# Projected blocks leave PSUM by a copy on ACT, and DVE's rotary steps read the copy in two parts

## The chip, the cores and the metric

One core of one Trainium2 chip. The metric is the device time of one execution in microseconds (us). The kernel before: 2270.76 us, the median of 3 runs (2270.74 to 2271.02). A shorter time is better.

The engines are named as in the profile: PE (TensorE, matmuls) with PEld (its weight loads), DVE (VectorE), ACT (ScalarE), POOL (GpSimd) and SP (SyncE, here the queue that issues the DMAs).

## The reference

4 x 1024 tokens of width 256 go through three stages, each added to its input: half an expert layer, attention, half the same expert layer again.

```
x = x + 0.5 * experts(layernorm(x))
x = x + attention(layernorm(x))
x = x + 0.5 * experts(layernorm(x))

experts:   32 experts of inner width 96, silu(gate) * up, then down; top 8 by softmax,
           cut where the renormalised sum passes 0.8, the weights renormalised
attention: q = x Wq^T (16 heads of 16), k = x Wk^T, v = x Wv^T (4 heads of 16)
           q = q * cos + rotate_half(q) * sin ; k the same      (v is not rotated)
           softmax(q k^T / 4) v, then Wo^T
```

All tensors are float32. The rotary step pairs each element of the first half of a head with one of the second half.

## The kernel before, in words

Everything is one long order of 384 slots, written out per engine. A slot d is one pair of expert chunks for a group of 512 tokens: PE computes gate and up (L1211) for slot d + 1 and down (L1229) for slot d - 1. 24 slots make a group, 192 a layer. Each float32 product is made of three float16 passes (high x high, high x low, low x high). The token groups of the first expert layer are also projected for attention, one group after another: in group k, slot s = d mod 24, three *join* events project group g = k - 1: first keys and values in one block (64 + 64 rows), then two blocks of queries (128 rows each). They stand in slots 8, 10, 13 for the first two groups and in 10, 12, 14 for the other six (join_slots).

From slot 64 on, *visits* are woven in: each gives PE two score matmuls for the row maxima (L1241, halves of 512 keys) and two for the exponentials (L1253), DVE two maxima (L960, one per half, each frees the bank of the next score matmul of its half), ACT two exponentials (L691). A slot has two or three visits. Every second visit or so PE also does a set of value matmuls (L1274).

The order in a slot, PE: gate, visit, up, visit, down, (visit), event. DVE: maxima of the first visit, gated (L937, once tanh is there), product (L945), maxima of the second visit, normalisation and routing pieces that the slot number names, event. POOL: low part of the hidden block (L606), rotary low part (L588), weighting by the expert weights (L601, released by the product). ACT: tanh (L668), exponentials, high part (L675), rotary high part (L682), exponentials.

PSUM has 8 banks, all in use. An event of PE writes its result into bank 7 early in the kernel and, while the value matmuls hold that bank (slots 79 to 311), into the bank of up (B_U) or gate (B_G). So the next up-projection waits for whoever reads the event's result (`taken`).

A join before the change, on DVE at the end of its slot (function join, L910 to L927): for the first block a transpose of the values out of PSUM (L918); then the cosine product into rb (L922) and the two sine products with halves swapped into turned (L923, L925), all three with the PSUM block as one operand and a table in SBUF as the other. The third one signals j_taken, which frees the bank. In the middle of the next slot, after the product, the sum rb + turned (L932) signals rope_done. One slot later ACT takes the high float16 part of rb (L682) and POOL the low part (L588), which signals qo_lo_done; then SP stores both. rb and turned are single buffers, so a join waits for qo_lo_done of the one before. In group slots 6, 7, 9 and 11 DVE has four normalisation pieces for the next group; the one in slot 11 is four operations of L839 (norm, piece 3). SP loads the cosine and sine tables of group g in slot 1 (function tables).

Of the kernel before, what the change touches and what calls it, by code (L numbers as in the profile page):

```python
# [7 lines left out]
ALU = mybir.AluOpType  # L8
ACT = mybir.ActivationFunctionType
# [6 lines left out]
P = 128  # L16
# [17 lines left out]
K_ROWS = KV * HD  # L34
# [82 lines left out]
JOINS = QB + 1  # L117
# [13 lines left out]
def join_slots(k):  # L131

    return () if k not in range(1, GROUPS + 1) else (8, 10, 13) if k - 1 in JOINS_BY_PE else (10, 12, 14)
# [66 lines left out]
def build(nc, x, wgu, wd, wg, wq, wk, wv, wo, ident_c, ktab_c, kneg_c, out):  # L200
    with ExitStack() as ctx:
# [32 lines left out]
        turned = sb("turned", [P, GROUP])  # L234
# [55 lines left out]
        v_turned = vb_f[K_ROWS:, :]  # L290
# [17 lines left out]
        PS = ctx.enter_context(nc.psum_tensor("PS", [P, 8, 512], F32))  # L308
# [10 lines left out]
        def bank16(b):  # L319
# [33 lines left out]
        j_done, j_taken, rope_done, qo_hi_done, qo_lo_done = (  # L353
            sem("j_done"), sem("j_taken"), sem("rope_done"), sem("qo_hi_done"), sem("qo_lo_done"))
        v_set, tab_in, vb_out, qo_out = sem("v_set"), sem("tab_in"), sem("vb_out"), [sem(f"qo_out{i}") for i in range(JOINS)]
# [37 lines left out]
        def _(sp):  # L393
# [4 lines left out]
            for k in range(2 * KT):  # L398
                n = n_gu // (2 * KT)
# [44 lines left out]
            def tables(g):  # L444

                cols = slice(g % 2 * GROUP, g % 2 * GROUP + GROUP)
                if g:
                    sp.wait_ge(j_taken, JOINS * g)
                for t, v in enumerate((kcos, ksin)):
                    sp.dma_start(v, ktab_c[t, :, cols]).then_inc(tab_in, 16)  # L450

# [189 lines left out]
        def _(act):  # L641
# [52 lines left out]
            def event(d, i):  # L694

                bank = event_bank(d, i)
                name, n, j = EVENTS[d][i]
                if name in ("p_hi", "p_lo"):
                    take_rows(norm_of_join(n), n % 2, name == "p_lo", bank)
                if name in ("t_hi", "t_lo"):  # L700
                    take_rows(norm_of_group(n), n % 2, name == "t_lo", bank)
# [64 lines left out]
        def _(dve):  # L766
# [140 lines left out]

            HALF = 2.0 ** 3 / XW

            def join(g, piece, bank):  # L910
                dve.wait_ge(j_done, JOINS * g + piece + 1)
                J = PS[:, bank, :]
                n, m = P if piece else K_ROWS, JOINS * g + piece
                if piece == 0:
                    dve.wait_ge(tab_in, 32 * (g + 1))
                    if g:
                        dve.wait_ge(vb_out, g * 64)
                    dve.transpose(v_turned, J[K_ROWS:, :]).then_inc(v_set, 1)  # L918
                if m:
                    dve.wait_ge(qo_lo_done, m)  # L920
                link.many((
                    dve.scalar_tensor_tensor(rb[0:n, :], J[0:n, :], HALF, kcos[0:n, :], ALU.mult, ALU.mult),  # L922
                    dve.scalar_tensor_tensor(turned[0:n // 2, :], J[n // 2:n, :], -HALF, ksin[n // 2:n, :],  # L923
                                             ALU.mult, ALU.mult)))
                dve.scalar_tensor_tensor(turned[n // 2:n, :], J[0:n // 2, :], HALF, ksin[0:n // 2, :],  # L925
                                         ALU.mult, ALU.mult).then_inc(j_taken, 1)
                dve.wait_ge(v_set, g + 1)  # L927

            def rope_sum(g, piece):
                n, m = P if piece else K_ROWS, JOINS * g + piece  # L930
                dve.wait_ge(j_taken, m + 1)
                dve.tensor_tensor(rb[0:n, :], rb[0:n, :], turned[0:n, :], ALU.add).then_inc(rope_done, 1)  # L932

            def gated(d):
# [92 lines left out]
            def event(d, i):  # L1027

                bank = event_bank(d, i)
                name, n, j = EVENTS[d][i]  # L1030
                if name == "logits":
                    route(n, 0, bank)
                if name == "join":
                    join(n, j, bank)
                if name == "out_y":
                    add_outputs(n, j, bank)

# [57 lines left out]
            for d in range(-1, SLOTS + 2):  # L1095
                k, s = divmod(d, PER_GROUP)
                if d % PER_HALF == 1 and d > 1:
                    add_dense(d // PER_HALF - 1)
                if (d, 0) in VISIT:
                    visit(VISIT[d, 0])  # L1100
                if d + 1 < SLOTS:
                    gated(d + 1)
                    product(d + 1)
                if (d, 0) in VISIT:
                    unit_ends(VISIT[d, 0])
                if s - 1 in join_slots(k):
                    rope_sum(k - 1, join_slots(k).index(s - 1))
                if d == -1 or d == 0:
                    split_piece(1, d + 1)
                if d in D_LOW_AT:  # L1110
                    split_d(D_LOW_AT.index(d) + 1)
                if d in (2, 3, 5, 6):
                    split_piece(2 + d // 5, (d - 2) % 3)
                if d == 8:
                    split_small()
                if d == SPLIT_BY - 1:
                    dve.memset(vst_f, 0.0).then_inc(ones_set, 1)
                    dve.wait_ge(ones_set, 1)
                    dve.memset(vst[:, :, :, HD:HD + 1], XW / 2.0 ** 6).then_inc(ones_set, 1)
                if (d, 1) in VISIT:  # L1120
                    visit(VISIT[d, 1])
                if len(EVENTS[d]) > 1:
                    event(d, 1)
                if (d, 2) in VISIT:
                    unit_ends(VISIT[d, 1])
                    visit(VISIT[d, 2])
                if d in OUT_AT:
                    normalise(OUT_AT.index(d))
                if d - 2 in OUT_AT:
                    turn_back(OUT_AT.index(d - 2))  # L1130
                if 1 <= k <= GROUPS and 2 <= s < 6:
                    if s == 2:
                        dve.wait_ge(x_done, 2 * k)
                    norm(norm_of_join(k - 1), k - 1, s - 2, k + 1)
                if 0 <= k < PREPS - 1:
                    if s in steps_of_norm(k)[0]:
                        norm_of(k + 1, steps_of_norm(k)[0].index(s))
                    if s == T_LOGITS + 1:
                        route(k + 1, 1)
                        route(k + 1, 2)  # L1140
                    if s == T_LOGITS + 2:
                        route(k + 1, 3)
                        route(k + 1, 4)
                    if s == T_LOGITS + 3:
                        route(k + 1, 5)
                        route(k + 1, 6)
                if EVENTS[d]:
                    event(d, 0)
                if (d, 2) in VISIT:
                    unit_ends(VISIT[d, 2])  # L1150
                elif (d, 1) in VISIT:
                    unit_ends(VISIT[d, 1])
# [282 lines left out]
```

## Time and profile before

| | us |
|---|---|
| median of 3 runs | 2270.76 |
| the profiled execution | 2270.94 |
| its span, first to last instruction | 2269.1 |
| PE busy | 2200.3 (97%) |
| DVE busy | 1626.9 (72%) |
| ACT busy | 1166.9 (51%) |
| POOL busy | 1072.5 (47%) |

Busy is the time in which an engine has at least one instruction running; the ends of matmuls are modelled. TensorE's granted clock is full speed over the whole span but for its first moments. An idle time of an engine counts only where PE, which is busy nearly all the time, waits for it in the end.

### The profile page before, as it was taken

How to read it: one execution, taken by the hardware profiler on the slowest of the kernel's cores; microseconds unless marked ns; L12 is line 12 of the kernel's file. 1: busy time of each engine (PE TensorE's matmuls, PEld its weight loads, DVE VectorE, ACT ScalarE, POOL GpSimd, SP SyncE). 2: the span in 40 equal slices, each digit the busy share in tenths (PEclk: the TensorE clock that was granted, in tenths of full speed). 3: DMA queues.
4: the chain of work that ended last, by engine and by line, in shares of the span. 5: the costliest groups of instructions: out<-in, count | busy, mean ns of one | idle time of the engine just before them, and what ended most of it. 6: DMA issues, size and time to landing. Idle time of an engine off the chain costs nothing.

```text
span 2269.1 us, 47149 instructions
## 1 busy us (share of the span) xinstructions
PE 2200.3 (97%) x18794; PEld 1487.7 (66%) x18794; DVE 1626.9 (72%) x3203; ACT 1166.9 (51%) x1885; POOL 1072.5 (47%) x908
## 2 busy tenths in 40 slices
PE   3999999999999999999999999999999999999998
PEld 2888875556565565565566566566655665688887
DVE  7756678887887877787877877777777754454543
ACT  4433331666556556565556565566656556433332
POOL 1767654444444444444434443434344334466655
PEclk9999999999999999999999999999999999999999
DMA  5211121011111120110211111010110110101010
GB/s 222 80 41 37 39 58 31 23 42 31 35 31 43 33 51 25 34 37 24 53 41 32 31 36 32 20 42 16 26 47 6 29 32 20 30 26 40 22 40 20
DMA packets 157956, 88.50 MB, mean 39 GB/s; under 512 B 103588, under 2 KB 149924, under 8 KB 156968
## 3 DMA queue, kind: packets, MB, share of 16 engines
q1 hardware_dynamic: 157592, 85.45, 14.1%
q8 instruction: 148, 2.42, 0.4%
q14 instruction: 72, 0.59, 0.1%
q10 hardware_dynamic: 144, 0.03, 0.0%
HBM read 63.14 MB, written 11.80 MB: 33 GB/s over the span
## 4 chain that ended last, share of the span: by engine, by line
PE 89%; DVE 7%; DMA 1%; issue 1%; ACT 1%; POOL 1%; SPq 0%; POOLq 0%; DVEq 0%
PE PS L1211 43%; PE PS L1229 21%; PE PS L1241 11%; PE PS L1274 10%; DVE arena L960 2%; PE PS L1193 1%; PE PS L1303 1%; DMA X<-wd 1%; PE PS L1253 1%; DVE arena L937 1%; DVE arena L945 1%; PE PS L1179 0%; DVE turned L923 0%; DVE turned L925 0%; DVE arena L922 0%
## 5 line engine op out<-in xcount | busy, mean ns | idle before, releaser
L1211 PE MATMUL PS<-XT,WGU 128*128 128x256 f16 x9216 | 1112.0, 273 | 14.2 <-DVE turned L925 8.8
L1211 PEld LDWEIGHTS PS<-XT,WGU 128*128 128x128 f16 x9216 | 875.9, 98 | 236.9 <-issue 129.9
L606 POOL TENSOR_TENSOR arena<-arena 128x512 f16<-128x512 f32 x384 | 451.2, 1175 | 1065.9 <-ACT arena L675 1065.9
L960 DVE TENSOR_REDUCE arena<-PS 128x1 f32<-128x512 f32 x1024 | 656.5, 684 | 269.3 <-PE PS L1241 265.4
L691 ACT ACTIVATE arena<-PS,fac 128x512 f32<-128x512 f32 x1024 | 647.4, 685 | 270.7 <-PE PS L1253 270.5
L668 ACT ACTIVATE arena<-PS,fac 128x512 f32<-128x512 f32 x384 | 264.4, 689 | 771.7 <-PE PS L1211 771.7
L1229 PE MATMUL PS<-WD,arena 128*128 128x256 f16 x4608 | 568.3, 273 | 2.6 <-POOL arena L606 2.4
L601 POOL TENSOR_TENSOR arena<-arena 128x512 f32<-128x512 f32 x384 | 501.7, 1306 | 85.9 <-DMA arena<-ce_scratch 44.5
L1229 PEld LDWEIGHTS PS<-WD,arena 128*128 128x128 f16 x4608 | 430.4, 98 | 145.6 <-issue 94.6
L937 DVE SCALAR_TENSOR_TENSOR arena<-arena,PS 128x512 f32<-128x512 f32 x384 | 261.2, 680 | 247.4 <-ACT arena L668 246.6
L1241 PE MATMUL PS<-arena 48*128 48x512 f16 x1024 | 318.9, 382 | 14.9 <-DVE arena L960 12.8
L1253 PE MATMUL PS<-arena 50*128 50x512 f16 x1024 | 315.9, 382 | 0.0
L945 DVE SCALAR_TENSOR_TENSOR arena<-arena,PS 128x512 f32<-128x512 f32 x384 | 263.8, 687 | 29.7 <-PE PS L1211 12.8
L675 ACT ACTIVATE arena<-arena 128x512 f16<-128x512 f32 x384 | 242.0, 630 | 16.1 <-POOL arena L601 15.9
L1274 PE MATMUL PS<-arena 128*32 128x512 f32 x2048 | 246.2, 598 | 0.0
L1241 PEld LDWEIGHTS PS<-arena 48*128 48x128 f16 x1024 | 62.1, 94 | 216.6 <-issue 124.7
L1274 PEld LDWEIGHTS PS<-arena 128*32 128x32 f32 x2048 | 53.4, 109 | 103.6 <-issue 93.4
L1253 PEld LDWEIGHTS PS<-arena 50*128 50x128 f16 x1024 | 63.6, 93 | 15.1 <-issue 10.9
L583 POOL TENSOR_TENSOR XS<-XN,XS 128x1024 f16<-128x1024 f32 x23 | 49.0, 2131 | 0.0
L839 DVE TENSOR_SCALAR XN<-X,mv,rstd 128x256 f32<-128x256 f32 x96 | 43.8, 517 | 0.0
L843 DVE BATCH_NORM_STATS2 stats<-X 128x6 f32<-128x256 f32 x96 | 33.4, 411 | 3.1 <-DMA X<-x 3.1
L1303 PE MATMUL PS<-WO,arena 128*128 128x256 f16 x256 | 33.3, 273 | 0.2 <-DVE arena L937 0.2
(117 smaller groups left out, 729.5 us busy)
## 6 DMA issues: line engine op xcount, KB each, us to landing
arena<-ce_scratch SPq DMA_DIRECT2D x256, 128.0 KB, 3.2
arena<-wgu SPq DMA_DIRECT2D x4, 1536.0 KB, 13.4
arena<-q_scratch SPq DMA_DIRECT2D x192, 32.0 KB
arena<-ktab_c SPq DMA_DIRECT2D x16, 256.0 KB, 4.0
q_scratch<-arena SPq DMA_DIRECT2D x32, 128.0 KB, 1.8
out<-X SPq DMA_DIRECT2D x8, 512.0 KB, 3.0
X<-wd SPq DMA_DIRECT2D x2, 1536.0 KB, 24.0
X<-x SPq DMA_DIRECT2D x1, 3072.0 KB, 12.1
```

Source lines behind the costliest of these rows:

```text
L601: pool.tensor_tensor(t, t, c, ALU.mult).then_inc(w_done, 1)
L606: pool.tensor_tensor(hs[1][:, d % HS, :], tw[d % 2], hs[0][:, d % HS, :], ALU.subtract).then_inc(lo_done, 1)
L668: act.activation(z_f, PS[:, B_G, :], ACT.Tanh, scale=F_TANH).then_inc(z_done, 1)
L691: act.activation(pex[:, v % RING * 2 + half, :], PS[:, B_EXP + half, :], ACT.Exp, scale=F_EXP).then_inc(exp_done, 1)
L937: dve.scalar_tensor_tensor(z_f, z_f, 1.0, PS[:, B_G, :], ALU.add, ALU.mult).then_inc(v_done, 1)
L945: dve.scalar_tensor_tensor(tw[d % 2], z_f, G_U_UP, PS[:, B_U, :], ALU.mult, ALU.mult).then_inc(t_done, 1)
L960: dve.tensor_reduce(mx[:, half * REP * QT + c:half * REP * QT + c + 1], PS[:, B_MAX + half, :], AX_X, ALU.max).then_inc(max_taken, 1)
L1211: ins = pe.matmul(PS[:, b, j * HALF_G:(j + 1) * HALF_G], WGU[w][:, kt, part * CHUNKS + c + j, :], XT[r][:, k % 2, kt, half * HALF_G:(half ...
L1229: ins = pe.matmul(PS[:, B_Y, i * HID:(i + 1) * HID], hs[r][:, d % HS, at:at + P], WD[w][:, d % PER_HALF * 2 + j, :], start=(first and j == ...
L1241: pe.matmul(PS[:, B_MAX + half, :], qst[64 * par:64 * par + 48, slot, i, t * P:(t + 1) * P], kst[64 * par:64 * par + 48, slot, half * 512: ...
L1253: pe.matmul(PS[:, B_EXP + n % 2, :], kst[64 * par:64 * par + 50, slot, k * P:(k + 1) * P], qst[64 * par:64 * par + 50, slot, head // 2, ha ...
L1274: ins = pe.matmul(PS[32 * head:32 * head + 32, B_O, :], vst[:, u % 2, k, :], pex[:, (2 * q + r // 2) % RING * 2 + r % 2, :], start=(k == 0 ...
```

## The change

ACT copies the whole block from PSUM into rb, at the event's place in its own order, and signals j_taken. DVE no longer has a join at the end of the slot. In the middle of the next slot, where the sum stood, DVE now computes the two sine products from rb (rope_partners); at the end of that next slot, after the event, it transposes the values out of rb (first block), multiplies rb by the cosine in place and adds turned (rope_sum). SP's table load waits for rope_done instead of j_taken.

```diff
@@ sync: tables(g)
-                    sp.wait_ge(j_taken, JOINS * g)
+                    sp.wait_ge(rope_done, JOINS * g)
@@ scalar: event(d, i)
+                if name == "join":
+                    m = JOINS * n + j
+                    act.wait_ge(j_done, m + 1)
+                    if m:
+                        act.wait_ge(qo_lo_done, m)
+                    act.activation(rb, PS[:, bank, :], ACT.Copy).then_inc(j_taken, 1)
@@ vector
-            def join(g, piece, bank):
-                dve.wait_ge(j_done, JOINS * g + piece + 1)
-                J = PS[:, bank, :]
+            def rope_partners(g, piece):
                 n, m = P if piece else K_ROWS, JOINS * g + piece
+                dve.wait_ge(j_taken, m + 1)
                 if piece == 0:
                     dve.wait_ge(tab_in, 32 * (g + 1))
+                link.many((
+                    dve.scalar_tensor_tensor(turned[0:n // 2, :], rb[n // 2:n, :], -HALF, ksin[n // 2:n, :],
+                                             ALU.mult, ALU.mult),
+                    dve.scalar_tensor_tensor(turned[n // 2:n, :], rb[0:n // 2, :], HALF, ksin[0:n // 2, :],
+                                             ALU.mult, ALU.mult)))
+
+            def rope_sum(g, piece):
+                n = P if piece else K_ROWS
+                if piece == 0:
                     if g:
                         dve.wait_ge(vb_out, g * 64)
-                    dve.transpose(v_turned, J[K_ROWS:, :]).then_inc(v_set, 1)
-                if m:
-                    dve.wait_ge(qo_lo_done, m)
-                link.many((
-                    dve.scalar_tensor_tensor(rb[0:n, :], J[0:n, :], HALF, kcos[0:n, :], ALU.mult, ALU.mult),
-                    dve.scalar_tensor_tensor(turned[0:n // 2, :], J[n // 2:n, :], -HALF, ksin[n // 2:n, :],
-                                             ALU.mult, ALU.mult)))
-                dve.scalar_tensor_tensor(turned[n // 2:n, :], J[0:n // 2, :], HALF, ksin[0:n // 2, :],
-                                         ALU.mult, ALU.mult).then_inc(j_taken, 1)
-                dve.wait_ge(v_set, g + 1)
-
-            def rope_sum(g, piece):
-                n, m = P if piece else K_ROWS, JOINS * g + piece
-                dve.wait_ge(j_taken, m + 1)
+                    dve.transpose(v_turned, rb[K_ROWS:, :]).then_inc(v_set, 1)
+                    dve.wait_ge(v_set, g + 1)
+                link(dve.scalar_tensor_tensor(rb[0:n, :], rb[0:n, :], HALF, kcos[0:n, :], ALU.mult, ALU.mult))
                 dve.tensor_tensor(rb[0:n, :], rb[0:n, :], turned[0:n, :], ALU.add).then_inc(rope_done, 1)
@@ vector: event(d, i)
-                if name == "join":
-                    join(n, j, bank)
@@ vector: the slot loop, after gated, product and unit_ends
                 if s - 1 in join_slots(k):
-                    rope_sum(k - 1, join_slots(k).index(s - 1))
+                    rope_partners(k - 1, join_slots(k).index(s - 1))
@@ vector: the slot loop, after the event
+                if s - 1 in join_slots(k):
+                    rope_sum(k - 1, join_slots(k).index(s - 1))
```

## Rows read from the trace of the kernel before

**Rows 1.** The page: span and PE's busy time.
```profile
span 2269.1 us, 47149 instructions
...
PE 2200.3 (97%) x18794; PEld 1487.7 (66%) x18794; DVE 1626.9 (72%) x3203; ACT 1166.9 (51%) x1885; POOL 1072.5 (47%) x908
```
**Rows 2.** PE's waits, 400 to 1320 us: total, times, longest.
```profile
PE PS L1211 <- DVE turned L925: 8.8, 13, 1.2
PE PS L1241 <- DVE arena L960: 7.8, 20, 0.9
```
**Rows 3.** All waits: DVE's for the projection matmuls.
```profile
DVE arena L922 <- PE PS L1193: 16.5, 14, 1.8
...
DVE arena L918 <- PE PS L1193: 7.9, 7, 1.8
```
**Rows 4.** The page's groups, tanh on ACT: busy us, mean ns, idle before.
```profile
L668 ACT ACTIVATE arena<-PS,fac 128x512 f32<-128x512 f32 x384 | 264.4, 689 | 771.7 <-PE PS L1211 771.7
```
**Rows 5.** Timeline 603 to 617 us, DVE then PE: start us, length us.
```profile
603.04 0.72 DVE L918 STREAM_TRANSPOSE arena<-PS 64x512 f32<-64x512 f32 x1 [1.02 <-PE PS L1193]
...
605.93 1.29 DVE L960 TENSOR_REDUCE arena<-PS 128x1 f32<-128x512 f32 x2
...
612.67 1.28 DVE L960 TENSOR_REDUCE arena<-PS 128x1 f32<-128x512 f32 x2
...
604.24 0.39 PE L1241 MATMUL PS<-arena 48*128 48x512 f16 x1
...
606.05 1.47 PE L1211 MATMUL PS<-XT,WGU 128*128 128x256 f16 x12 [1.20 <-DVE turned L925]
...
614.75 0.38 PE L1241 MATMUL PS<-arena 48*128 48x512 f16 x1
```
**Rows 6.** Timeline 1098 to 1108 us, DVE then PE.
```profile
1099.11 1.29 DVE L960 TENSOR_REDUCE arena<-PS 128x1 f32<-128x512 f32 x2 [0.69 <-PE PS L1241]
...
1105.32 1.27 DVE L960 TENSOR_REDUCE arena<-PS 128x1 f32<-128x512 f32 x2
...
1106.65 0.39 PE L1241 MATMUL PS<-arena 48*128 48x512 f16 x1 [0.21 <-DVE arena L960]
```
**Rows 7.** Timeline 188 to 191 us; then line L601: min/median/max ns.
```profile
188.27 0.68 DVE L932 TENSOR_TENSOR arena<-arena,turned 64x512 f32<-64x512 f32 x1
188.43 1.65 POOL L601 TENSOR_TENSOR arena<-arena 128x512 f32<-128x512 f32 x1 [0.62 <-DVE arena L945]
188.87 1.22 DVE L852 TENSOR_TENSOR nw<-rs 128x4 f32<-128x4 f32 x1
...
190.12 0.16 DVE L853 TENSOR_TENSOR nw<-nw,var 128x4 f32<-128x4 f32 x1
...
L601 POOL TENSOR_TENSOR arena<-arena x384: 1256/1269/2789, 49.9 to 2260.2; 128x512 f32<-128x512 f32 x192
```
**Rows 8.** Timeline 1263 to 1275 us, DVE then PE.
```profile
1263.57 1.29 DVE L960 TENSOR_REDUCE arena<-PS 128x1 f32<-128x512 f32 x2 [0.69 <-PE PS L1241]
...
1271.67 1.29 DVE L960 TENSOR_REDUCE arena<-PS 128x1 f32<-128x512 f32 x2
...
1274.20 0.38 PE L1241 MATMUL PS<-arena 48*128 48x512 f16 x1
```
**Rows 9.** Timeline 1130 to 1136 us (a third block), DVE then PE.
```profile
1130.77 1.08 DVE L932 TENSOR_TENSOR arena<-arena,turned 128x512 f32<-128x512 f32 x1
1131.77 2.47 DVE L960 TENSOR_REDUCE arena<-PS 128x1 f32<-128x512 f32 x4
1135.26 1.29 DVE L960 TENSOR_REDUCE arena<-PS 128x1 f32<-128x512 f32 x2 [1.02 <-PE PS L1241]
...
1133.10 0.39 PE L1241 MATMUL PS<-arena 48*128 48x512 f16 x1 [0.21 <-DVE arena L960]
```
**Rows 10.** Timeline 620 to 629 us (a second block), PE then DVE.
```profile
620.80 0.38 PE L1211 MATMUL PS<-XT,WGU 128*128 128x256 f16 x2 [0.47 <-DVE turned L925]
...
628.02 1.29 DVE L960 TENSOR_REDUCE arena<-PS 128x1 f32<-128x512 f32 x2 [1.65 <-PE PS L1241]
```

## The prediction

> **What bounds the kernel now.** I read the page first: PE is busy in 2200.3 of 2269.1 us [rows 1]. So only what holds PE up can move the time, and the next view is PE's waits inside the stretch where attention runs beside the expert slots (400 to 1320 us) [rows 2]. The gate/up matmuls wait 8.8 us in 13 places for DVE's last rotary step (L925), because a projected block lies in the bank that the next up-projection wants. The score matmuls wait another 7.8 us in 20 places for DVE's row maxima (L960): so DVE runs close to PE's pace here, and a delay of DVE turns into a delay of PE. Third, DVE's own waits: 24.4 us for the projection matmuls, in 21 places [rows 3].
>
> **What goes.** The ACT copy takes over the release of the bank. Its price is a 128x512 PSUM read on ACT, 0.69 us by the tanh of the same shape, and ACT is idle before that tanh (771.7 us over the kernel, ended by the gate matmuls) [rows 4]. The next gate matmuls alone take some 1.5 us after the projection (twelve of them 1.47 [rows 5]), so the copy is finished before the up matmuls start: the 8.8 us go. Six of these stalls are followed by a 0.1 us stall of a score matmul that goes with them (no row shown): -9.4 us at most. I put the copy at 0, hidden by ACT's wait for the gate matmuls; without that cover it would be 0.7 us for each of the 18 blocks that share a bank with them, 13 us. The extra wait in front of the copy (qo_lo_done) is one DVE had at the same place; behind it on ACT stands the next tanh. It was met in time before and I cost it at 0. The table load of SP waits for rope_done instead of j_taken: it has ten slots to spare, 0.
>
> **What moves on DVE.** Per block three operations of some 0.7 us (for the first block of a group a transpose of 0.72 too [rows 5]) ran at the end of the projection's slot, in time in which DVE had little else, since PE was doing the projection and the gate. Now two of them stand in the middle of the next slot, and the others with the sum at its end. No work is saved: five instructions before, five after (four for a later block). What changes is that DVE can't begin them until it has done the next slot's first maxima, gate and product. I write M0 for the first maxima of the slot after that; PE's second score matmul of the visit that follows needs both.
>
> *First block of a group, third query-time group (603 to 617 us).* [rows 5] Four operations, 603.04 to 605.93, 2.9 us. The first maxima start at 605.93, though their scores were written at 604.24 + 0.39 = 604.63: 1.3 us of that is won back when the operations leave. They come back before M0: so M0 at 612.67 moves by 2.9 - 1.3 = 1.6 us, plus the collision below (0.9): 2.5 us. The M0 pair then ends at 612.67 + 2.5 + 1.28 = 616.45, and PE's second score matmul, which began at 614.75, can't begin before 616.5. That is +1.8 us at this place, the saved 1.2 us stall [rows 5] already inside, because I compare clock times. The cause is that this slot also holds the four normalisation steps of L839, so DVE has no idle time between the two rows of maxima.
>
> *The worst case (1099 to 1107 us).* [rows 6] Here DVE waited 0.69 us for the scores before its first maxima: the rotary steps had been wholly hidden, nothing is won back. M0 moves by 2.9 + 0.9 = 3.8 us from 1105.32 to 1109.1, ends at 1110.4, and PE's second score matmul was at 1106.65: +3.8 us.
>
> **The collision.** The rotary steps used to read one operand from PSUM. From the copy, the three products read two SBUF tensors, as the sum L932 already did. The trace shows what this does beside POOL [rows 7]: L932 starts at 188.27; POOL's weighting L601, released by the product just before, takes 1.65 us where its median is 1.27 (it begins after L932 is through); and the next all-SBUF DVE operation, L852 on 4 columns, takes 1.22 us where its neighbour L853 of the same size takes 0.16: it ends with L601, at 190.09. Now the two partner steps stand exactly there, behind the product. The first takes L932's part, the second L852's: it ends about 0.5 us (0.69 less 0.16) after L601, at 190.6, where two free steps would end at 188.27 + 2 x 0.69 = 189.65. So 0.9 us more for each of 24 blocks. Ends: 0 (if the second step wins against POOL) and 1.5 us (L932 itself was held to 1.08 us in one place, where another POOL operation was in flight [rows 9], so 0.4 more, and 0.2 for a hit at the cosine step now and then, a guess). I take 0.9, the nearest row. Where unit_ends' small steps stand between the product and the partners (one group), POOL gets through beforehand: 0 there.
> The Trainium skill, SBUF — State Buffer, section Who interferes with whom, says that a DVE instruction with two SBUF inputs and a GpSimd instruction that reads SBUF exclude each other for a whole instruction, whichever started first; the trace agrees in the three rows just read. By a per-operation reading of that rule alone every one of the three steps could be held; by the rows only the one behind another is.
>
> **The sum.** First blocks, six groups in the attention stretch: 1.8 and 3.8 from above; the last group, DVE idle before its maxima as in the worst case, M0 at 1271.67 + 3.8, end 1276.75, PE's second score matmul at 1274.20: +2.6 [rows 8]. Three more of the pattern, read in the same way: +1.7, +1.6 (the one without a collision) and +0.6 (DVE has 1.2 us of idle time in that stretch). Together +12.1.
> Second blocks: the stall of 0.47 us goes and M0 is late by 1.6 + 0.9 less what is won back (1.2), while DVE was idle 1.65 us there [rows 10]: nearly covered. The six give from -0.3 to +0.5, I take +0.6 together.
> Third blocks: only 0 to 0.5 us is won back. In the worst-shaped one the sum was held to 1.08 us by POOL, two partner steps with the second behind L601 come to 0.7 + 0.9 = 1.6 us more, and PE's score matmul waits already (at 1133.10, after 0.21 us): +1.6 [rows 9]. The others by the same reading: +2.1, +0.8, +0.7, +0.6, -0.5. Together +5.3, of which I keep 4.3, as DVE's idle time behind (1.02 us [rows 9]) takes part of it.
> The two groups before attention starts: DVE waits for a projection 24.4 / 21 = 1.2 us on the mean [rows 3] and lets it pass, but here PE's slot has no visits and is short, so gate waits for gated now and then; between 0 and 2 us each, I take 1, together 2.
> Sum: 12.1 + 0.6 + 4.3 + 2.0 = +19.0 us. The profiled execution took 2270.94 us, 0.18 over the median 2270.76. Forecast 2289.8, say 2290 us.
>
> **Rivals.**
> *A, the moved work finds room (faster).* The mechanism: DVE is no longer late for the first maxima, PE reaches the next slot earlier, and the idle time that DVE has in it (24.4 us were spent waiting for projections [rows 3]) absorbs the five steps. Then the 9.4 us go and nothing comes: 2261.5. For it: DVE is busy 72% only, and the idle times of 0.69 to 1.65 us [rows 6, 10]. Against it: between the two rows of maxima of rows 5 DVE has none. It decides if less than half of the first-block lateness appears, which needs M0 to be late by under 1 us.
> *B, no collision.* The second partner step wins against POOL or reads no shared path. Then every first block is 0.9 cheaper (five of them, 4.5), the second and third blocks about 8 together, and the early groups 1: 19.0 - 13.5 = +5.5, so 2276.4. Against it: L852 behind L601 [rows 7].
> *C, ACT becomes late too.* rope_high stands on ACT before the next slot's second pair of exponentials and now waits for a sum that comes 2.5 to 3.8 us later; the score matmuls for exp would wait 0.5 to 1 us in each first block: +5 on top, 2295.
> By the same page of the Trainium skill (SBUF — State Buffer, Who interferes with whom) the loser of a collision waits the whole of the other's instruction: were each of the three steps a loser, an estimate would be a further 1.2 us in the crowded slots, still under C's end.
> A rival that the change doesn't do what it says I don't see: the bank is released by a semaphore on another engine, and that is all it needs.
>
> **Chances.** Forecast case (2283 to 2294) 0.55; A 0.12; B and cases between B and the forecast (2273 to 2283) 0.25; C 0.08. Faster by over 0.2% (4.5 us, about what can be told from no change): A, 0.12. Within it: what of B lies under 2275.3, 0.12. Slower: 0.76. The range reaches down to 2271, where A's lesser forms begin, and up to 2297.
>
> **What would show it.** No wait of L1211 for a rotary step; ACT copy near 0.69 us; one partner step near 0.7 and the other near 1.6 us; PE's wait for L960 between 400 and 1320 us up from 7.8 to some 25 to 35 us, with stalls of 1.5 to 4 us at a first block's second slot. I am wrong if the partner steps both take 0.7 us (B), or if L960 stalls stay under 15 us (A).

## The result: 2332.3 us, slower by 2.7%

| | before | after |
|---|---|---|
| median | 2270.76 us | 2332.3 us (2330.35 to 2333.22, 5 runs) |
| the profiled execution | 2270.94 us | 2332.3 us |
| its span | 2269.1 us | 2330.5 us |
| PE busy | 2200.3 us | 2222.4 us |

The ratio is 1.027, 95% interval [1.0255, 1.0285]. The forecast was 2290 us, at most 2297: the direction was right, and the loss is 61.5 us where 19 were forecast.

PE's waits of the whole kernel, after: total, times, longest.

```profile
PE PS L1246 <- DVE arena L965: 51.0, 78, 3.1
...
PE PS L1216 <- DVE arena L942: 12.4, 11, 2.8
```

L965 is the row maximum (L960 before), L942 is gated (L937 before). In the trace of before the same two waits over the whole kernel are 12.8 and 2.3 us; the wait for the third rotary step, 8.8 us in 13 places [rows 2], is gone. So PE waits 38.2 + 10.1 - 8.8 = 39.5 us longer. That is not all of the 61.5. The rest is in the clock. The core row (span, mean granted clock) was 1.000 before and is now:

```profile
core 0: 2330.5 us, clock 0.992
```

0.8% of 2330.5 us is 19 us. Stretches of the trace of after around two equal stalls of PE show where it goes (the columns are the stretch, its length, busy us of PE, PEld, DVE, ACT, POOL, then the granted clock, DMA share, GB/s):

```profile
205.00:209.00 4.00, 3.82 (x20) 2.80 (x21) 2.08 (x4) 2.34 (x4) 3.73 (x3) 0.57 0.28 89
312.00:316.00 4.00, 3.64 (x34) 3.27 (x35) 3.02 (x5) 2.63 (x4) 3.56 (x3) 1.00 0.33 101
```

Both start at the end of a stall of 2.8 us behind gated, as PE's timeline of after shows:

```profile
205.18 1.18 PE L1216 MATMUL PS<-XT,WGU 128*128 128x256 f16 x6 [2.78 <-DVE arena L942]
...
312.36 0.83 PE L1216 MATMUL PS<-XT,WGU 128*128 128x256 f16 x6 [2.79 <-DVE arena L942]
```

After the first, TensorE ran at the lower level, 1.2 GHz, for most of 4 us and did 20 matmuls; after the second it stayed at 2.4 GHz and did 34. The trace has eleven such stretches of 3.4 us inside the span, each beginning within 2 us of the end of a stall of PE of 1.4 to 3.1 us. Of the 18 stalls of that length between 180 and 1360 us, the other seven brought none. The trace of before has neither such a stall nor such a stretch there (in both traces the clock falls once more in the last 2 us, as the work ends). At half speed each costs 1.7 us, 18.8 in all. 39.5 + 18.8 = 58.3 of the 61.5 us; the last 3 us I did not trace.

The worst case of before [rows 6], after the change, DVE (start us, length us):

```profile
1137.72 1.29 DVE L965 TENSOR_REDUCE arena<-PS 128x1 f32<-128x512 f32 x2 [4.05 <-PE PS L1246]
...
1140.96 0.68 DVE L924 SCALAR_TENSOR_TENSOR turned<-arena 32x512 f32<-32x512 f32 x1
1141.67 1.64 DVE L926 SCALAR_TENSOR_TENSOR turned<-arena 32x512 f32<-32x512 f32 x1
1143.35 1.29 DVE L965 TENSOR_REDUCE arena<-PS 128x1 f32<-128x512 f32 x2
1144.55 1.37 DVE L845 TENSOR_SCALAR XN<-X,mv,rstd 128x256 f32<-128x256 f32 x4
1145.96 0.71 DVE L934 STREAM_TRANSPOSE arena<-arena 64x512 f32<-64x512 f32 x1
1146.70 1.47 DVE L936 SCALAR_TENSOR_TENSOR arena<-arena 64x512 f32<-64x512 f32 x1
1148.20 0.68 DVE L937 TENSOR_TENSOR arena<-arena,turned 64x512 f32<-64x512 f32 x1
1148.81 1.27 DVE L965 TENSOR_REDUCE arena<-PS 128x1 f32<-128x512 f32 x2
```

POOL in the same stretch, and PE's score matmuls that wait for the two pairs of maxima:

```profile
1141.01 1.76 POOL L601 TENSOR_TENSOR arena<-arena 128x512 f32<-128x512 f32 x1 [0.18 <-DVE arena L950]
1146.48 1.15 POOL L606 TENSOR_TENSOR arena<-arena 128x512 f16<-128x512 f32 x1 [3.70 <-ACT arena L675]
...
1144.10 0.39 PE L1246 MATMUL PS<-arena 48*128 48x512 f16 x1 [1.51 <-DVE arena L965]
...
1149.55 0.39 PE L1246 MATMUL PS<-arena 48*128 48x512 f16 x1 [3.05 <-DVE arena L965]
```

Read it from the product's end, 1140.9. The first sine product (L924) takes 0.68 us. POOL's weighting L601, released by the product, stretches from 1.27 to 1.76 us. The second sine product (L926) ends 0.5 us after L601, as forecast. But the cosine product (L936) too takes 1.47 us, beside L606, which starts 0.2 us before it. DVE has no idle moment between the first maxima and 1150, and PE loses 1.51 + 0.21 us and then 3.05 + 0.21 us.

The rotary steps of all blocks (ns: min/median/max; L924 and L926 the sine products, L937 the sum, L936 the cosine product, L703 the ACT copy):

```profile
L924 DVE SCALAR_TENSOR_TENSOR turned<-arena x24: 680/1026/1193, 187.3 to 1354.3; 64x512 f32<-64x512 f32 x16, 32x512 f32<-32x512 f32 x8
L926 DVE SCALAR_TENSOR_TENSOR turned<-arena x24: 681/1642/1658, 188.2 to 1355.5; 64x512 f32<-64x512 f32 x16, 32x512 f32<-32x512 f32 x8
L937 DVE TENSOR_TENSOR arena<-arena,turned x24: 683/692/1527, 193.0 to 1359.1; 128x512 f32<-128x512 f32 x16, 64x512 f32<-64x512 f32 x8
...
L936 DVE SCALAR_TENSOR_TENSOR arena<-arena x24: 648/682/1470, 192.3 to 1358.4; 128x512 f32<-128x512 f32 x16, 64x512 f32<-64x512 f32 x8
...
L703 ACT ACTIVATE arena<-PS x24: 597/597/598, 183.8 to 1350.1; 128x512 f32<-128x512 f32 x24
```

To place the loss I compared the start of each slot's gate matmuls in both traces. The growth of the difference, by block and its next slots, sums to 61.3 us:

| | forecast (us) | measured (us) | of it clock stretches, number: x 1.7 us | without them |
|---|---|---|---|---|
| first blocks, six later groups | 12.1 | 27.6 | 5: 8.5 | 19.1 |
| second blocks | 0.6 | 8.6 | 2: 3.4 | 5.2 |
| third blocks | 4.3 | 12.5 | 3: 5.1 | 7.4 |
| the two groups before attention | 2.0 | 12.6 | 1: 1.7 | 10.9 |
| sum | 19.0 | 61.3 | 11: 18.7 | 42.6 |

### The profile page after: what moved, and what is told of

The parts are those of the page before. It is cut to its first block, busy times and chain, and to the rows that moved or that the text cites. A ratio compares the mean times of both kernels' runs of the same rounds, so it can differ in the third digit from the quotient of the medians.

```text
span 2330.5 us, 47175 instructions
## 1 busy us (share of the span) xinstructions
PE 2222.4 (95%) x18794; PEld 1494.6 (64%) x18794; DVE 1662.0 (71%) x3203; ACT 1181.7 (51%) x1909; POOL 1073.1 (46%) x908
## 4 chain that ended last, share of the span: by engine, by line
PE 83%; DVE 12%; issue 2%; DMA 1%; ACT 1%; POOL 1%; SPq 0%; POOLq 0%; DVEq 0%; ACTq 0%
PE PS L1216 40%; PE PS L1234 19%; PE PS L1246 10%; PE PS L1279 9%; DVE arena L965 3%; DVE turned L926 2%; DVE arena L942 1%; PE PS L1198 1%; PE PS L1308 1%; DMA X<-wd 1%; PE PS L1258 1%; DVE turned L924 1%; DVE arena L950 1%; DVE XN L845 1%; DVE arena L936 0%
## 5 line engine op out<-in xcount | busy, mean ns | idle before, releaser
L606 POOL TENSOR_TENSOR arena<-arena 128x512 f16<-128x512 f32 x384 | 451.2, 1175 | 1097.7 <-ACT arena L675 1097.7
L965 DVE TENSOR_REDUCE arena<-PS 128x1 f32<-128x512 f32 x1024 | 656.3, 684 | 301.8 <-PE PS L1246 297.5
L601 POOL TENSOR_TENSOR arena<-arena 128x512 f32<-128x512 f32 x384 | 501.0, 1305 | 86.6 <-DMA arena<-ce_scratch 44.7
L942 DVE SCALAR_TENSOR_TENSOR arena<-arena,PS 128x512 f32<-128x512 f32 x384 | 260.8, 679 | 262.1 <-ACT arena L668 261.5
L1258 PEld LDWEIGHTS PS<-arena 50*128 50x128 f16 x1024 | 64.7, 93 | 15.0 <-issue 10.9
L845 DVE TENSOR_SCALAR XN<-X,mv,rstd 128x256 f32<-128x256 f32 x96 | 44.4, 524 | 0.1
L703 ACT ACTIVATE arena<-PS 128x512 f32<-128x512 f32 x24 | 14.3, 597 | 48.8 <-PE PS L1198 46.2
L926 DVE SCALAR_TENSOR_TENSOR turned<-arena 64x512 f32<-64x512 f32 (+1 forms) x24 | 38.5, 1603 | 0.7
## 6 DMA issues: line engine op xcount, KB each, us to landing
arena<-wgu SPq DMA_DIRECT2D x4, 1536.0 KB, 13.5
```

What stands on the lines that cost most here:

```text
L601: pool.tensor_tensor(t, t, c, ALU.mult).then_inc(w_done, 1)
L606: pool.tensor_tensor(hs[1][:, d % HS, :], tw[d % 2], hs[0][:, d % HS, :], ALU.subtract).then_inc(lo_done, 1)
L942: dve.scalar_tensor_tensor(z_f, z_f, 1.0, PS[:, B_G, :], ALU.add, ALU.mult).then_inc(v_done, 1)
L965: dve.tensor_reduce(mx[:, half * REP * QT + c:half * REP * QT + c + 1], PS[:, B_MAX + half, :], AX_X, ALU.max).then_inc(max_taken, 1)
L1258: pe.matmul(PS[:, B_EXP + n % 2, :], kst[64 * par:64 * par + 50, slot, k * P:(k + 1) * P], qst[64 * par:64 * par + 50, slot, head // 2, ha ...
```

## The experiments

**One-input steps in the same places.** The three products of the changed kernel become transposes of the same shapes, which read one SBUF tensor; the rotation is left out, and the constant HALF goes into the scale of ACT's copy.

```diff
-                    dve.scalar_tensor_tensor(turned[0:n // 2, :], rb[n // 2:n, :], -HALF, ksin[n // 2:n, :], ...),
-                    dve.scalar_tensor_tensor(turned[n // 2:n, :], rb[0:n // 2, :], HALF, ksin[0:n // 2, :], ...)))
+                    dve.transpose(turned[0:n // 2, :], rb[n // 2:n, :]),
+                    dve.transpose(turned[n // 2:n, :], rb[0:n // 2, :])))
...
-                link(dve.scalar_tensor_tensor(rb[0:n, :], rb[0:n, :], HALF, kcos[0:n, :], ALU.mult, ALU.mult))
+                link(dve.transpose(rb[0:n, :], rb[0:n, :]))
```

> The changed kernel with the two sine products and the cosine product replaced by 32x32 transposes of the same shapes, which read one SBUF tensor instead of two (so the rotation is left out; the copy scales the block by the constant instead). Places, order and waits are the same. Theory (collisions with POOL are over half of the loss): each of the three takes 0.7 us, PE's waits for the row maxima and for gated fall from 63 to 25 to 38 us, fewer stretches at the half clock, time 2280 to 2298. Rival (the place alone, DVE's work pushed into the crowded slot, whatever its operands): 2315 or more. Rival (ACT, whose rotary high part waits for the late sum): 2320 or more.

2290.46 us (2288.76 to 2291.37); ratio to before 1.0085 [1.0068, 1.0101]. The steps that stand in for the sine products:

```profile
L924 DVE STREAM_TRANSPOSE turned<-arena x24: 699/706/707, 187.3 to 1316.4; 64x512 f32<-64x512 f32 x16, 32x512 f32<-32x512 f32 x8
L925 DVE STREAM_TRANSPOSE turned<-arena x24: 701/705/707, 188.0 to 1317.1; 64x512 f32<-64x512 f32 x16, 32x512 f32<-32x512 f32 x8
```

Not one of the 48 is held by POOL. PE's wait for the maxima:

```profile
PE PS L1244 <- DVE arena L963: 30.5, 61, 2.9
```

41.8 of the 61.5 us are gone: what goes with the second SBUF operand is two thirds of the loss, its share of the clock stretches included. Four stretches are left of eleven, one of them twice as long (6.8 us): 8.5 us instead of 18.8. PE's waits for the maxima and for gated (4.4 us here) are 28.5 us shorter together, and the clock gives back 10.3: of the 41.8 us this accounts for 38.8. The place alone costs the other 20. The two early groups, 12.6 us in the changed kernel, cost 2.3 us here.

**Only the sine products one-input.** The same without the second change of that diff.

> As the run before, but only the two sine products are transposes; the cosine product stays a product of two SBUF tensors. Theory: the second sine product behind POOL's weighting is the main collision, the cosine product mostly runs when POOL is idle: within 5 us of the run before. Rival (every all-SBUF product is hit alike): a third of the way back to 2332, so 15 us above the run before.

2292.47 us (2291.66 to 2294.02), 2 us above the run before. So nearly all of it hangs on the pair behind the product. The cosine product costs little, though it is as long as in the changed kernel:

```profile
L934 DVE SCALAR_TENSOR_TENSOR arena<-arena x24: 647/682/1468, 190.3 to 1319.4; 128x512 f32<-128x512 f32 x16, 64x512 f32<-64x512 f32 x8
```

So it is not the pair that pushes it into POOL's next operation; its place does that, in two blocks of 24 (0.88 and 1.47 us in both kernels).

**One sine product in the middle, one at the end.** All operands as in the change.

```diff
@@ rope_partners
-                link.many((first sine product, second sine product))
+                link(first sine product)
@@ rope_sum, in front of the cosine product
+                link(second sine product)
```

> The changed kernel with one sine product in the middle of the next slot and the other one moved to its end, in front of the cosine product. The same instructions, operands and copy; only no two all-SBUF products stand back to back behind the product that releases POOL's weighting. Theory (that pair is what POOL splits): the second sine product takes 0.7 us instead of 1.64, the first some 0.7 to 1.1, and the time comes to 2290 to 2305. Rival (any all-SBUF product in the crowded slot meets POOL as often): 2320 or more.

2308.53 us (2307.72 to 2310.04), ratio to before 1.0167 [1.0152, 1.0182]. The first and the second sine product:

```profile
L923 DVE SCALAR_TENSOR_TENSOR turned<-arena x24: 680/1029/1199, 187.2 to 1333.5; 64x512 f32<-64x512 f32 x16, 32x512 f32<-32x512 f32 x8
L933 DVE SCALAR_TENSOR_TENSOR turned<-arena x24: 680/685/1640, 190.6 to 1336.0; 64x512 f32<-64x512 f32 x16, 32x512 f32<-32x512 f32 x8
```

Taking the pair apart gives back 24 us, and the second product is at 0.69 us in 18 of 24 blocks. It is above my 2290 to 2305. The first product still meets POOL's L606 (1.03 us), and in the two early groups nothing came back (12.0 us lost there, 12.6 in the changed kernel). There the second product still takes 1.4 to 1.6 us in four blocks of six, and behind the first product POOL now holds what stands there instead (L858 ends with L601; of the four L845, one meets L601 and one L606):

```profile
188.10 1.11 DVE L858 TENSOR_TENSOR nw<-rs 128x4 f32<-128x4 f32 x1
...
199.05 3.14 DVE L845 TENSOR_SCALAR XN<-X,mv,rstd 128x256 f32<-128x256 f32 x4
```

In the changed kernel these take 0.16 us and 2.22 us.

**The copy alone, with all products at the old place.**

```diff
@@ vector: event(d, i), with the copy on ACT as in the change
+                if name == "join":
+                    rope_partners(n, j)      # the two sine products, from rb
+                    rope_cos(n, j)           # transpose and cosine product, from rb
@@ the next slot
                 if s - 1 in join_slots(k):
                     rope_sum(...)            # the sum alone, as before
```

> The ACT copy as in the change, but DVE does transpose, sine and cosine products from the copy at the old place, the end of the projection's slot, and the sum in the middle of the next slot as before. Theory (the loss comes from where DVE does its work and what it meets there, not from the copy): the bank stalls of 8.8 us go, DVE ends its products 0.8 us later than before, and PE waits that time for row maxima instead: 2266 to 2278. Rival (copy or SBUF operands cost by themselves, wherever they stand): 2290 or more.

2285.07 us (2284.12 to 2285.33), ratio 1.0063 [1.0048, 1.0078]: between the two bounds that I had written, nearer to the theory. The bank stall is gone, and PE waits 26.4 us for maxima instead of 12.8. The copy stands in front of DVE's products, which in most blocks end 0.6 to 1.0 us later, and PE meets DVE one wait later. What I had not expected: 5.6 us of the 14 are lost in the two early groups, where they end 0.9 to 1.4 us later. And the operands cost something here too. In one of the second blocks the first product waits out a long POOL operation and the cosine product meets L606:

```profile
953.82 2.72 DVE L924 SCALAR_TENSOR_TENSOR turned<-arena 64x512 f32<-64x512 f32 x1 [1.31 <-ACT arena L703]
953.87 2.12 POOL L583 TENSOR_TENSOR XS<-XN,XS 128x1024 f16<-128x1024 f32 x1
...
957.29 1.54 DVE L936 SCALAR_TENSOR_TENSOR arena<-arena 128x512 f32<-128x512 f32 x1
```

PE then waits 2.0 us for a maximum, and one of this run's two stretches at the lower clock follows: 3.6 us of the 14 lie behind this block.

**Without the products.** The changed kernel with the three products left out, all else kept (turned holds zeros, and ACT's copy has the constant as its scale).

```diff
-                link.many((first sine product, second sine product))
...
-                link(cosine product)
```

> The changed kernel with the three rotary products of DVE left out (the copy, the value transpose, the sum and all waits stay, turned holds zeros). Theory (all of the loss is DVE being late): the bank stalls are gone and DVE has 2.1 us less per block: 2256 to 2264, no wait of PE for a maximum over 1 us after a projection beyond those of before. Rival (ACT's copy or its wait for the sum delays exponentials or tanh): over 2270.

2264.69 us (2263.93 to 2265.69), ratio 0.9974 [0.9964, 0.9985]: 6 us below the kernel before, 0.7 us above the theory's range. No harm shows from the copy on ACT and from ACT's order. ACT's wait for the sum, 29.2 us in the changed kernel, is 3.4 us here: it follows DVE's lateness. Even so, in four groups the second slot behind the first block takes 0.8 to 3.1 us longer than before (the 3.1 with a stretch at the lower clock in it): in the slot in front of it the transpose and the sum stand at the end, with the normalisation. The longest wait for a maximum is 1.6 us, where my theory had none above 1.

**Projections one slot later**, in the changed kernel and in the kernel before.

```diff
-    return () if k not in range(1, GROUPS + 1) else (8, 10, 13) if k - 1 in JOINS_BY_PE else (10, 12, 14)
+    return () if k not in range(1, GROUPS + 1) else (8, 10, 13) if k - 1 in JOINS_BY_PE else (11, 13, 15)
```

> The changed kernel with the projections of the six later groups one slot later (11, 13, 15 for 10, 12, 14), so that the moved steps no longer share a slot with the last normalisation piece. Theory (the first blocks lose most because the five moved steps and the normalisation piece fall into one slot): the first blocks' loss of 3 to 6.5 us each comes down to that of the later blocks (1 to 3), in all 2305 to 2322. Rival (collisions with POOL are all of it, the slot doesn't matter): 2326 or more.

> The kernel before with the same shift of the projections. It tells what the shift does by itself. Theory: the stall of the bank stays, the idle time of DVE after the projection stays: 2267 to 2275. Rival (the normalisation piece in the same slot was a help as it stood before the projection): over 2276.

The changed kernel comes to 2317.12 us (2314.88 to 2320.24), the kernel before to 2281.24 us (2279.8 to 2283.32): the shift costs the kernel before 10.5 us, against my theory, because now the normalisation stands in front of the rotary steps and holds the bank (PE waits 18.5 us for L925 instead of 8.8, 2.9 at the longest). The changed kernel gains 15.2 us by the same shift, in the range of the theory. The early groups, which the shift doesn't touch, still lose 12.5 us, so some 15 of the 49 us that the six later groups lose go with the slot that they share with the normalisation. Between the two shifted kernels the change costs 35.9 us instead of 61.5, but this makes the share look larger than it is: 9.7 us of the difference are bank stalls that the shift adds to the kernel before, and that the copy takes away.

**Filled stalls.** Matmuls into a free bank in front of four of the gate waits of the early groups.

```diff
@@ gate_or_up(d, part)
+                if part == 0 and d in (36, 38, 60, 62):
+                    for i in range(6 if d in (36, 60) else 12):
+                        pe.matmul(PS[:, B_EXP, :], ident[:, :], XT[0][:, k % 2, 0, :], start=True, stop=True)
```

> The changed kernel with 6, 12, 6 and 12 matmuls of 512 columns into a bank that nobody uses yet, put in front of the four gate waits that stall PE 1.4 and 2.8 us in the first two groups (before attention starts). They add 36 matmuls of 0.21 us, 7.7 us, inside 8.4 us of stalls. Theory (a PE stall also brings a stretch at the half clock, which costs 1.7 us more): the stretch that the changed kernel shows near 205 us is gone, the four stalls are filled, and the time is the changed kernel's or up to 2 us under it: 2329 to 2333. Rival (the half clock there has nothing to do with the stall): the stretch stays, or the fillers add their 7.7 us.

2329.17 us (2328.68 to 2330.63). The stretch that had the clock at 0.57, now:

```profile
205.00:209.00 4.00, 3.83 (x35) 3.44 (x36) 2.83 (x5) 2.45 (x4) 3.74 (x3) 1.00 0.28 89
```

35 matmuls instead of 20, at 2.4 GHz. From there on each slot's gate starts 1.70 us earlier than in the changed kernel, and nowhere else in the kernel is there a difference of more than 0.15 us from slot to slot. The 36 added matmuls cost nothing. So this stretch did follow from the stall, and it has a price of its own; the other ten were not taken away one by one. (The medians differ by 3.1 us, more than this; the changed kernel's runs spread over 2.9 us.)

**A version that is faster.** In the kernel before, ACT copies only what shortens DVE's way to the bank's release: the value rows (first block), and the lower half of the block into the rows that the second sine product writes. DVE's cosine and first sine product still read PSUM at once, and the first sine product now signals j_taken.

```diff
@@ scalar: event(d, i)
+                if name == "join" and j == 0:
...                                              # waits for the projection and for rb to be free
+                    act.activation(rb[K_ROWS:, :], PS[K_ROWS:, bank, :], ACT.Copy).then_inc(j_copied, 1)
+                if name == "join":
+                    half = (P if j else K_ROWS) // 2
+                    act.wait_ge(cos_done, JOINS * n + j + 1)
+                    act.activation(turned[half:2 * half, :], PS[0:half, bank, :], ACT.Copy).then_inc(low_in, 1)
@@ vector: join(g, piece, bank)
+                if piece == 1:
...
+                    dve.transpose(v_turned, rb[K_ROWS:, :]).then_inc(v_set, 1)     # not in the first block any more
...
-                dve.scalar_tensor_tensor(turned[n // 2:n, :], J[0:n // 2, :], HALF, ksin[0:n // 2, :],
-                                         ALU.mult, ALU.mult).then_inc(j_taken, 1)
+                dve.wait_ge(low_in, m + 1)
+                link(dve.scalar_tensor_tensor(turned[n // 2:n, :], turned[n // 2:n, :], HALF, ksin[n // 2:n, :],
+                                              ALU.mult, ALU.mult))
```

The value rows alone:

> The kernel before, where ACT copies only the value rows (partitions 64 to 127) of a group's first block out of PSUM while DVE starts at once with the cosine product of the key rows; DVE transposes the values from the copy at the next projection's place, where it is idle. Theory (DVE's instructions in front of the bank's release are what costs, and idle DVE time before a projection is free): three stalls of 1.2 us become 0.47, the first maxima come 0.7 us sooner: 2264 to 2269. Rival (the copy beside DVE's read of the same bank slows either): 2271 or more.

2271.31 us (2269.9 to 2271.41), ratio 1.0 [0.9991, 1.0009]: no change, and the theory (2264 to 2269) missed. Three stalls became 0.8 us shorter each; the transpose in front of the next projection cost 0.4 and 0.9 us in two groups, where DVE was not idle after all. Six of the ten executions show a mean clock of 0.999 and take 2271.3 us or a little more; the other four, at 1.000, take 2269.9 to 2270.4. The rival, that copy and product slow each other at the same bank, is not the cause: side by side they take 0.59 and 0.68 us (first two rows of the trace below).

With the lower half:

> The run before with one thing more: while DVE does the first sine product, ACT copies the lower half of the block into the rows that the second sine product will write, and DVE does that product in place from SBUF right behind, when POOL is idle. The bank is free after two DVE steps. Theory: nine or more stalls of 0.47 us and six of 0.1 us go as well, and no collision comes: 2259 to 2266. Rival (DVE waits for the copy or for POOL, so its products end later than before and the maxima with them): no better than the run before.

2269.46 us (2269.35 to 2269.69), ratio 0.9994 [0.9985, 1.0004]: above the theory's 2259 to 2266 too. The wait for the third rotary step is gone, but the two early groups lost 1 us each, as PE waited for the copy at the up matmuls, whose bank is another one there. That wait moved to the next use of the bank:

> The earlier version in which ACT copies the value rows and the lower half, with PE's wait for that copy moved, for the first two groups, from the next up matmuls to the next use of that bank. Theory: the 2 us that these two groups lost go: 2266.5 to 2268.5. Rival (they were lost to the second sine product's place): 2269 or more.

2267.04 us (2266.94 to 2267.33), ratio 0.9984 [0.9975, 0.9994]: 3.6 us faster than before, as the theory had it, and the fastest of all versions that compute the whole reference. One first block in it, 600 to 606 us, ACT and DVE, then PE:

```profile
602.41 0.59 ACT L703 ACTIVATE arena<-PS 64x512 f32<-64x512 f32 x1 [1.57 <-PE PS L1207]
602.41 0.68 DVE L934 SCALAR_TENSOR_TENSOR arena<-PS,arena 64x512 f32<-64x512 f32 x1 [1.02 <-PE PS L1207]
603.12 0.68 DVE L936 SCALAR_TENSOR_TENSOR turned<-PS,arena 32x512 f32<-32x512 f32 x1
603.13 0.59 ACT L707 ACTIVATE turned<-PS 32x512 f32<-32x512 f32 x1
603.84 0.68 DVE L940 SCALAR_TENSOR_TENSOR turned<-turned,arena 32x512 f32<-32x512 f32 x1
604.16 1.48 PE L1228 MATMUL PS<-XT,WGU 128*128 128x256 f16 x12
604.55 1.29 DVE L974 TENSOR_REDUCE arena<-PS 128x1 f32<-128x512 f32 x2
```

The up matmuls start 1.95 us after the gate matmuls (602.21 to 604.16); in the kernel before it was 3.2 us (602.84 to the 606.05 of [rows 5]), and the all-SBUF product at 603.84 takes 0.68 us: POOL has nothing running beside it (its next operation starts at 606.18).

The transpose three slots later, in place:

> As the run before, but ACT copies the value rows into the buffer of the transposed values and DVE transposes it in place three slots later, where DVE waits for scores, instead of in front of the next projection. Theory: the 0.4 and 0.9 us that two groups lost behind that transpose go as well: 2265 to 2267.5. Rival (SP, which must wait for the transposed values before its next loads, comes late): 2268 or more.

2268.17 us (2268.04 to 2268.42), 1.1 us slower than that and outside the theory's 2265 to 2267.5: the 0.9 us came back, but 0.4 us in each early group and 1.0 in another were lost.

## Why the prediction was wrong

The direction was right, and the chain of causes as far as it went; the size was 42.3 us short in the table above. 18.7 us of that are the clock, for which the sum had no term, 8.9 the two early groups, 7.7 the second and third blocks and 7.0 the first blocks. Step by step:

- *What bounds it, and that DVE near PE's pace turns delay into stalls*: right. PE's new waits are for L965 and L942; apart from L925's, which is gone, no other wait changed by more than 0.3 us.
- *The copy at 0*: right. It takes 0.60 us, not 0.69, in time in which ACT was idle, and the kernel without products is faster than before. The 8.8 us went.
- *The collision*: right in kind. L601 goes between the two sine products and the second takes 1.64 us, as forecast. It was mis-sized: 0.9 us per block, which took L932's usual 0.68 us for the first product. That one has a median of 1.03 us, for in 22 of 24 blocks L606 was still in flight when it came. By their means (1.60 and 1.03 against 0.68 and 0.69 before) the pair takes 1.26 us more per block; 24 blocks make 30 us of DVE time, not 22. My upper end was 1.5. What this time costs PE was the larger miss: the prediction put what the collision adds at 13.5 us (rival B against the forecast), and the kernel with one-input steps puts it at 41.8, of which 10.3 are clock.
- *The sum, first blocks*: the first step that failed. I moved M0 and read what it did to one score matmul. I did not follow the rest: the maxima in front of it (1.51 us of PE's wait at 1144.10) and, in the worst case, the cosine product beside L606. Without the clock the three blocks with numbers of their own became 4.0, 4.8 and 4.5 us for 1.8, 3.8 and 2.6; all six, 19.1 for 12.1.
- *The two groups before attention*, "I take 1, together 2": 10.9. No slot was worked out. There are no scores there, but gated stands behind the rotary sum, and the gate matmuls wait for gated: 1.42 and 2.78 us here. DVE of the changed kernel, then PE:

```profile
188.16 1.64 DVE L926 SCALAR_TENSOR_TENSOR turned<-arena 32x512 f32<-32x512 f32 x1
...
193.03 0.68 DVE L937 TENSOR_TENSOR arena<-arena,turned 64x512 f32<-64x512 f32 x1
193.64 0.67 DVE L942 SCALAR_TENSOR_TENSOR arena<-arena,PS 128x512 f32<-128x512 f32 x1
...
194.37 2.79 PE L1216 MATMUL PS<-XT,WGU 128*128 128x256 f16 x24 [1.42 <-DVE arena L942]
```

- *Second and third blocks*: 4.9 forecast, 12.6 measured without the clock. I counted DVE's idle time as cover to its full length; a block whose steps take 1.2 us more uses it up.
- *The clock*: not in the prediction at all, 18.8 us, the largest single part of the miss. Rows of before showed it at full speed over the whole span, and I took that as given for a kernel whose PE would pause 3 us at a time.
- *Rival A* (the work finds room) fell. *Rival B* (no collision) was priced at 2276.4; the run without a second SBUF operand took 2290.5, so the place was under-priced too: 5.5 us, measured 20, of which the clock stretches are 8.5. *Rival C* (ACT late) is seen in ACT's 29.2 us wait for the sum, but no wait of PE for exponentials grew: it cost nothing that I could find.
- *Which steps are held*: I took only the one behind another. The trace of after has the first sine product over 0.8 us in 22 of 24 blocks, the cosine product at 0.88 and 1.47 us in two blocks and the sum at 1.53 us in three. By the Trainium skill, SBUF — State Buffer, Who interferes with whom, any DVE instruction with two SBUF inputs contends with a GpSimd instruction that reads SBUF; the trace agrees.

What stays open: why one stall of PE brings the lower clock and an equal one doesn't. The eleven stretches could be counted, but only one of them was taken away by itself, so the 1.7 us of each of the others is its length at half speed and not a measured difference.

## What to carry to other kernels

When a bank is the bottleneck, a copy on an idle engine is nearly free, but the operations that then read the copy have changed: here each got a second SBUF operand and stood beside POOL, and a pair of them behind the product that starts POOL cost more than the stall that the copy removed. Leave the operations that read PSUM where they are, and copy only the part that shortens the way to the release (-3.6 us here, against +61.5). Before moving work of an engine that keeps pace with PE, write out the slot it goes to in full, with every wait of PE in it, and the slots of each stage of the kernel, those that look easy too; and where the forecast has PE stalls of 2 us and more, add a price for the clock.

## What the runs showed of the hardware that was not expected

- TensorE fell to its lower clock level for 3.4 us behind a stall of 2.78 us in the first group, and not behind one of 2.79 us in the second. Filling the first with matmuls kept it at full speed.
- A 128x512 float32 copy from PSUM to SBUF on ACT takes 0.60 us, a tanh of the same shape 0.69 us.
- ACT reading partitions 64 to 127 of a PSUM bank and DVE reading partitions 0 to 63 of the same bank at the same time slowed neither (0.59 and 0.68 us, both from 602.41).
- A DVE product with two SBUF operands that meets a POOL operation in flight ends 0.54 to 0.55 us after it: the second sine product in 23 of 24 blocks, at 1.64 to 1.66 us behind L601, and the first in 22, at 0.82 to 1.19 us behind L606. POOL's L601, which starts after the first sine product does, still runs before the second. With one-input operations in their place none was held.
